# Sparse attention: the product with the sums' reciprocals by ScalarE, a head at a time, in place of VectorE

## The chip, the cores and the metric

One core of a Trainium2 chip runs the whole program. The metric is the device time in microseconds (us) of one execution. Engines: TensorE (PE, its weight loads PEld), VectorE (DVE), ScalarE (ACT), GpSimd (POOL) and SyncE (SP, which only issues DMAs here).

## The reference

The program is a macaron stack: expert layer, sparse attention, expert layer, expert layer, dense attention, expert layer. The change is in the sparse attention. Its core, for 8 batches of 256 tokens, 8 heads of 16 columns:

```python
scores = jnp.einsum('bhqd,bhkd->bhqk', Q, K) * scale
thr = jax.lax.top_k(scores, k)[0][..., k - 1:k]          # k = 25 of 256
masked = jnp.where(scores >= thr, scores, -jnp.inf)
probs = jax.nn.softmax(masked, axis=-1)
attn = jnp.einsum('bhqk,bhkd->bhqd', probs, V)
attn = attn.transpose(0, 2, 1, 3).reshape(B, S, D)
distilled = (attn.reshape(-1, g2) @ Wd.T + bd).reshape(B, S, D)
mixed = gate * distilled + (1.0 - gate) * attn
return mixed @ Wo.T + bo
```

The softmax is not divided before the product with V. V carries a column of ones beside each head's 16, so the product of the unnormalised weights gives a head's 16 sums and, in a 17th column, the sum of its weights. Division by that sum comes last: a reciprocal of 8 columns and a product of 8 x 16 columns by 8 reciprocals. The change is about this product.

## The kernel before, in words

Every engine has its own instruction stream, written out by hand, and waits for others by counting semaphores (dictionary `A` for this attention). An engine takes its stream in order: what waits holds up all behind it.

The attention (`pe_a0`, `act_a0`, `dve_a0`, `pool_a0`) goes in 64 steps `a`: a step is two heads of one half batch (128 queries), four steps make a half batch (`g`), eight a batch `b`. I write r0 to r7 for the steps of a batch (`r = a % 8`). For a step:

- PE computes the scores (`pe_a0_S`, L512), three steps ahead; ACT copies them out of PSUM (`act_a0_c`, L1105).
- DVE searches the 25th largest of each row (`dve_a0_topk`): for each of two heads four MAX8 (L1707) and three MATCH_REPLACE8 (L1709).
- POOL takes the row maximum for the exponential (`pool_a0_negm`, L2082), ACT does the exponential (`act_a0_e`, L1117), POOL the comparison with the threshold and the product (`any_select`, L1732, L1738). In most steps POOL also issues an indirect DMA of the expert layer (L2066 in the first 24 steps; L2051 in 33 to 40, 49 to 56 and from 59).
- PE transposes the weights a step later (L529), ACT copies them (`act_a0_pT`, L1123), PE multiplies them with V two steps later (`pe_a0_PV`, L543) into bank 2 or 3, by the half batch.

The end of a batch is done within the next one. On DVE, `dve_a0_nrm` stands ahead of the search in r1 (first half) and r3 (second half): a reciprocal into the single buffer `rden` (L1716) and the product into `attn` (L1718). On PE, `pe_a0_aT` transposes `attn` in r3 (L555), behind the scores of that step; `pe_a0_ds` in r4 (L560) and `pe_a0_o` in r5 (L566 to L568) give the layer's output. ACT stands between these with `act_a0_aT` (L1127) and `act_a0_mixt` (L1099). DVE adds the output to `x` in r7, ahead of that step's search (`dve_a0_x`, L1723). The next batch's projections run between: q in r2 (L471), k in r3 (L477), V in r4 (L483).

In order, PE's stream in step r3 is: scores of step r6, transposes of `attn`, transposes of step r2's weights, product of step r1, projection k. ACT's is: exponential of r3, copies of the scores of r6, copy of r2's weights, copy of k, copy of the transposed `attn`.

The last batch has its first half's reciprocal and product ahead of the search of step 63, and its second half's behind the last selection.

Of the kernel before, what the change touches and what calls it, by code (L numbers as in the profile page):

```python
# [6 lines left out]
P = 128  # L7
# [4 lines left out]
ACT = mybir.ActivationFunctionType  # L12

B, S, D = 8, 256, 128
# [9 lines left out]
H0, DH0 = 8, 16  # L24
# [35 lines left out]
def build(nc, packed, packed_b, x_in, out):  # L60
    ctx = ExitStack()
    with ctx:
        def sb(name, cols, dt=F32, rows=P):
            return ctx.enter_context(nc.sbuf_tensor(name, [rows, cols], dt))

        def sem(name):
            return ctx.enter_context(nc.semaphore(name))

        def sems(stage, names):
            return {n: sem(f"{stage}_{n}") for n in names.split()}  # L70

        def after(e, s, n):

            if n > 0:
                e.wait_ge(s, n)


        bank = [ctx.enter_context(nc.psum_tensor(f"bank{i}", [P, CN], F32)) for i in range(8)]
# [5 lines left out]
        def cst(name, a=0, b=None, rows=slice(0, P)):  # L84
# [17 lines left out]

        W = {"m0": dict(w1=0, w2=512, b2=768, b1=896, all=900), "m1": dict(w1=0, w2=256, b2=512, b1=640, all=642)}
        tab = {k: nc.dram_tensor(f"tab_{k}", (E * P, W[k]["all"]), F32).ap() for k in W}
        b2d = nc.dram_tensor("b2d", (E, D), F32).ap()

        xsc = nc.dram_tensor("xsc", (AREAS * BS, D), F32).ap()
        ys = nc.dram_tensor("ys", (NBLK * BS, D), F32).ap()
        ws = [sb(f"ws{n}", W["m0"]["all"]) for n in range(SLOTS)]
        xb = [sb(f"xb{n}", BS) for n in range(XSLOTS)]  # L110
# [63 lines left out]
        rden = sb("rden", H0)  # L174
        attn, aT, mixt = (s2b[:, n * S:n * S + S] for n in (0, 1, 3))
# [5 lines left out]
        s_b2d = sem("s_b2d")  # L181
        s_tab = {k: sem("s_tab_" + k) for k in W}
        s_mhalf, s_set, s_setup, s_late_done = (sem(n) for n in ("s_mhalf", "s_set", "s_setup", "s_late_done"))
# [18 lines left out]
        A = sems("a0", "stats mv veps rstd nmr xn T xT q qe k ke V Ve th gp gate S c tk negm e mask p PT pT PV den nrm "  # L202
                       "aT aTe ds wo1 mixt o x")
# [159 lines left out]
        def pe_dense_second(e, u, x_):  # L363
            n, w = u.x0 + x_, W[u.k]["w2"]
            e.wait_ge(F["hb"], u.j0 + 2 * x_ + 2)
            after(e, F["x"], n - 1)
            if x_ < 2:

                after(e, M["ye"], NBLK * u.i)
            for t in range(CT):  # L370
                for a in range(2):
                    i = e.matmul(bank[2 + x_ % 2][:, t * P:t * P + P],  # L372
                                 hbD[:, (2 * x_ + a) % 4 * CN + t * P:(2 * x_ + a) % 4 * CN + t * P + P],
                                 ws[(u.w0 + x_) % SLOTS][:, w + a * D:w + a * D + D], start=a == 0, stop=a == 1)
            i.then_inc(F["y"], 1)
# [30 lines left out]
        def pe_block_second(e, g, n):  # L406
            b = g.first + n
            w = W[g.k]["w2"]
            e.wait_ge(M["hb"], b + 1)
# [85 lines left out]
        def scores(a):  # L495

            return a + min(a, LEAD)
# [49 lines left out]
        def ebank(b):  # L547

            return bank[0 if b == B - 1 else 1]
# [495 lines left out]
        def act_a0_xT(e, b):  # L1045
            e.wait_ge(A["T"], b + 1)
            e.activation(axT[:, :], bank[0][:, 0:S], ACT.Copy, accum_out=xsum[:, :]).then_inc(A["xT"], 1)

        def act_a0_qe(e, b):
            e.wait_ge(A["q"], b + 1)  # L1050
            for n in range(2):
                i = e.activation(qT[b % 2][:, n * S:n * S + S], bank[0][:, n * S:n * S + S], ACT.Identity, bias=cst("a0_bq", n, n + 1))
            i.then_inc(A["qe"], 1)

        def act_a0_ke(e, b):
            e.wait_ge(A["k"], b + 1)
            for n in range(2):
                i = e.activation(kT[b % 2][:, n * S:n * S + S], bank[0][:, n * S:n * S + S], ACT.Identity, bias=cst("a0_bk", n, n + 1))
            i.then_inc(A["ke"], 1)

        def act_a0_xn(e, b):
            e.wait_ge(A["nmr"], 2 * b + 2)
            after(e, A["T"], b)
            for t in range(2):
                i = e.activation(xn[:, t * P:t * P + P], x[:, b * S + t * P:b * S + t * P + P], ACT.Identity,
                                 bias=rstd[:, 2 + t:3 + t], scale=rstd[:, t:t + 1])
            i.then_inc(A["xn"], 1)

        def act_a0_th(e, b):
            e.wait_ge(A["V"], b + 1)  # L1070
            e.activation(gsm[:, 0:1], bank[0][0:64, S:S + 1], ACT.Tanh, bias=bgh[:, 0:1], scale=0.5 / S).then_inc(A["th"], 1)
# [9 lines left out]
        def act_a0_gate(e, b):  # L1081
            e.wait_ge(A["gp"], b + 1)
            g = gate[b % 2]
            e.activation(g[:, 0:1], bank[0][:, 0:1], ACT.Identity, bias=cst("a0_bgp"))
            e.activation(g[:, 1:2], bank[0][:, 0:1], ACT.Identity, bias=gateb[:, 0:1], scale=-1.0)
            e.activation(g[:, 2:3], bank[0][:, 0:1], ACT.Identity, bias=gateb[:, 1:2], scale=cst("a0_bd")).then_inc(A["gate"], 1)
# [14 lines left out]
        def act_a0_c(e, a):  # L1101
            e.wait_ge(A["S"], scores(a) + 1)
            after(e, A["p"], a - 3)
            for j in range(2):
                i = e.activation(sS[:, (a % 4 * 2 + j) * S:(a % 4 * 2 + j + 1) * S], bank[4 + j][:, 0:S], ACT.Copy)  # L1105
            i.then_inc(A["c"], 1)
# [5 lines left out]
        def act_a0_e(e, a):  # L1112
            e.wait_ge(A["negm"], a + 1)
            after(e, A["p"], a - 1)
            for n in range(2):
                q, s = (a % 2 * 2 + n) * S, a % 4 * 2 * S + n * S
                i = e.activation(eS[:, q:q + S], sS[:, s:s + S], ACT.Exp, bias=negm[:, a % 2 * 2 + n:a % 2 * 2 + n + 1], scale=DH0 ** -0.5)  # L1117
            i.then_inc(A["e"], 1)

        def act_a0_pT(e, a):  # L1120
            e.wait_ge(A["PT"], a + 1)
            after(e, A["PV"], a - 1)
            e.activation(pT[:, a % 2 * 2 * S:(a % 2 + 1) * 2 * S], bank[6 + a % 2][:, :], ACT.Copy).then_inc(A["pT"], 1)  # L1123

        def act_a0_aT(e, b):
            e.wait_ge(A["aT"], b + 1)
            e.activation(aT[:, :], ebank(b)[:, 0:S], ACT.Identity, bias=gateb[:, 2:3]).then_inc(A["aTe"], 1)  # L1127
# [21 lines left out]
        def act_a0(e):  # L1149
            for a in range(8 * B):  # L1150
                b, r = a // 8, a % 8
                act_a0_e(e, a)
                if LEAD <= a + 3 < 8 * B:
                    act_a0_c(e, a + 3)
                if a >= 1:
                    act_a0_pT(e, a - 1)
                if b + 1 < B:
                    if r == 0:
                        act_a0_xn(e, b + 1)
                    elif r == 1:  # L1160
                        act_a0_xT(e, b + 1)
                    elif r == 2:
                        act_a0_qe(e, b + 1)
                    elif r == 3:
                        act_a0_ke(e, b + 1)
                    elif r == 4:
                        act_a0_th(e, b + 1)
                    elif r == 5:
                        act_a0_Ve(e, b + 1)
                    elif r == 7:  # L1170
                        act_a0_gate(e, b + 1)
                if r == 7:
                    act_a0_wo1(e, b)
                if b > 0 and r == 3:
                    act_a0_aT(e, b - 1)
                elif b > 0 and r == 4:
                    act_a0_mixt(e, b - 1)
                if a in NORM_A0:
                    act_xn(e, S1.parts[NORM_A0[a]])
                elif a in T_A0:  # L1180
                    act_xnT(e, S1.parts[T_A0[a]])
                elif a in TOP_A0:
                    act_th(e, S1.parts[TOP_A0[a]])
            act_a0_pT(e, 8 * B - 1)
# [524 lines left out]
                    e.match_replace(wk[:, n * S:n * S + S], m8s[:, m:m + 8], s, -3.0e38).then_inc(A["tk"], 1)  # L1709

        def dve_a0_nrm(e, b, g):
            W = DH0 + 1
            o = bank[2 + g][:, 0:H0 * W].rearrange("p (h d) -> p h d", h=H0)
            e.wait_ge(A["PV"], b * 8 + (g + 1) * 4)
            after(e, A["aT"], b)
            e.reciprocal(rden[:, :], o[:, :, DH0]).then_inc(A["den"], 1)  # L1716
            e.wait_ge(A["den"], 2 * b + g + 1)
            e.tensor_tensor(attn[:, g * P:g * P + P].rearrange("p (h d) -> p h d", h=H0), o[:, :, 0:DH0],  # L1718
                            rden[:, :].unsqueeze(2).to_broadcast([P, H0, DH0]), ALU.mult).then_inc(A["nrm"], 1)
# [678 lines left out]
```

## Time and profile before

| | us |
|---|---|
| three runs | 1114.26, 1118.98, 1119.06 |
| median | 1118.98 |
| the profiled execution | 1111.8 |
| its span | 1110.0 |
| DVE busy of the span | 789.5 (71%) |
| PE busy | 951.4 (86%) |
| ACT busy | 571.4 (51%) |
| POOL busy | 459.8 (41%) |

All times of rows are microseconds from the start of the span of the profiled execution, unless marked ns. An engine's instructions overlap a little: the next one starts before the one ahead has ended, so a chain's length is read from start to start. The sparse attention lies at about 190 to 525 us.

### The profile page before, as it was taken

What the parts mean: (1) busy time and instruction counts of PE and PEld (TensorE: products, weight loads), DVE (VectorE), ACT (ScalarE), POOL (GpSimd) and SP (SyncE); (2) the same over time, 40 slices, a digit from 0 to 9 for tenths busy, and PEclk for the clock granted to TensorE, in tenths of its full rate; (3) what the DMA queues carried; (4) which work ended last, traced back from release to release, by engine and by line L of the source; (5) the groups of instructions that cost most, each with busy time, mean ns of one, the idle gap of its engine ahead of it and who ended that gap; (6) DMA issues with size and microseconds to landing.
All of it is one profiled execution on the core that took longest, in us unless ns stands there. A gap on an engine that the chain in (4) does not pass through costs nothing.

```text
span 1110.0 us, 18262 instructions
## 1 busy us (share of the span) xinstructions
PE 951.4 (86%) x5092; PEld 723.8 (65%) x5092; DVE 789.5 (71%) x3096; ACT 571.4 (51%) x1309; POOL 459.8 (41%) x538
## 2 busy tenths in 40 slices
PE   5869979779798898875999785999899999997994
PEld 3538867567576776755995574885566666666963
DVE  5545687999999999995555853346688786864333
ACT  4326655445454544533763451677666766752631
POOL 2530028888757857845004435002522041032034
PEclk9979985555555555555999997999999999998998
DMA  9845613000150000012774313651100000005852
GB/s 306 290 143 148 207 40 134 11 12 15 29 75 8 13 1 6 13 57 91 209 214 139 86 32 94 179 160 34 32 9 1 1 20 2 1 20 151 245 160 61
DMA packets 63444, 95.66 MB, mean 86 GB/s; under 512 B 12128, under 2 KB 41968, under 8 KB 63216
## 3 DMA queue, kind: packets, MB, share of 16 engines
q1 hardware_dynamic: 46256, 71.94, 22.2%
q0 software_dynamic: 6144, 12.60, 3.8%
q10 hardware_dynamic: 10944, 9.97, 2.7%
q8 instruction: 42, 0.69, 0.3%
q14 instruction: 58, 0.48, 0.1%
HBM read 69.94 MB, written 30.83 MB: 91 GB/s over the span
## 4 chain that ended last, share of the span: by engine, by line
PE 43%; POOL 10%; issue 7%; ACT 4%; DVE 4%; another core or an unknown queue 3%; DMA 1%; POOLq 0%; ACTq 0%; SPq 0%; DVEq 0%
PE bank L764 9%; PE bank L403 6%; PE bank L748 5%; PE bank L416 4%; POOL vb L1732 4%; PE bank L360 3%; POOL hb L1738 3%; PE bank L738 3%; PE bank L372 2%; PE bank L732 2%; POOL yg L2066 2%; PE bank L543 1%; PE bank L391 1%; POOL xsc L2051 1%
## 5 line engine op out<-in xcount | busy, mean ns | idle before, releaser
L2066 POOL DMA_INDIRECT yg<-ys,posg x96 | 96.0, 1000 | 144.8 <-DMA ys<-ysb 55.5
L1707 DVE MAX8 vb<-sg 128x8 f32<-128x256 f32 x384 | 146.3, 431 | 0.0
L1732 POOL TENSOR_SCALAR vb<-sS,vb 128x256 f32<-128x256 f32 x126 | 115.2, 925 | 65.0 <-DVE vb L1707 61.6
L2051 POOL DMA_INDIRECT xsc<-xnS,posu x96 | 96.2, 1002 | 63.8 <-DVE posu L1481 35.9
L1117 ACT ACTIVATE hb<-sS,negm 128x256 f32<-128x256 f32 x128 | 58.0, 501 | 120.3 <-POOL negm L2082 119.9
L403 PE MATMUL bank<-xbT,ws 128*128 128x256 f32 x456 | 114.5, 388 | 0.0
L360 PE MATMUL bank<-xnT,ws 128*128 128x512 f32 x192 | 99.2, 646 | 13.6 <-issue 8.7
L543 PEld LDWEIGHTS bank<-kn,qn 128*128 128x128 f32 x512 | 107.0, 308 | 0.0
L1709 DVE MATCH_REPLACE8 sg<-vb,sg 128x256 f32<-128x256 f32 x256 | 104.9, 426 | 0.0
L543 PE MATMUL bank<-kn,qn 128*128 128x17 f32 x512 | 101.4, 338 | 0.0
L372 PEld LDWEIGHTS bank<-ws,hb 128*128 128x128 f32 x512 | 67.2, 206 | 49.7 <-issue 38.1
L372 PE MATMUL bank<-ws,hb 128*128 128x128 f32 x512 | 69.9, 291 | 32.5 <-issue 16.0
L529 PE MATMUL bank<-pk,hb 128*128 128x128 f32 x256 | 66.7, 413 | 35.3 <-POOL hb L1738 33.9
L403 PEld LDWEIGHTS bank<-xbT,ws 128*128 128x128 f32 x456 | 82.7, 195 | 9.3 <-issue 0.7
L529 PEld LDWEIGHTS bank<-pk,hb 128*128 128x128 f32 x256 | 47.5, 215 | 58.2 <-POOL hb L1738 48.6
L416 PEld LDWEIGHTS bank<-ws,hbM 128*128 128x128 f32 x608 | 79.3, 192 | 6.3 <-issue 1.7
L512 PE MATMUL bank<-zacc,exb 16*128 16x256 f32 x240 | 68.9, 669 | 15.9 <-ACT sS L1105 13.4
L1738 POOL TENSOR_TENSOR hb<-vb,hb 128x512 f32<-128x512 f32 x63 | 79.8, 1267 | 5.2
L1839 DVE SCALAR_TENSOR_TENSOR zacc<-bank,rden,zacc 128x128 f32<-128x128 f32 x256 | 78.0, 347 | 5.1
L416 PE MATMUL bank<-ws,hbM 128*128 128x128 f32 x608 | 79.7, 275 | 0.8 <-DVE ysb L1581 0.8
L764 PEld LDWEIGHTS bank<-VO,sS 128*128 128x128 f32 x512 | 63.1, 198 | 24.2 <-issue 15.1
L764 PEld LDWEIGHTS bank<-VO,hb 128*128 128x128 f32 x512 | 60.3, 191 | 24.5 <-issue 16.0
(226 smaller groups left out, 1913.3 us busy)
## 6 DMA issues: line engine op xcount, KB each, us to landing
ws<-tab_m SPq DMA_DIRECT2D x46, 450.0 KB, 3.7
ws<-tab_m SPq DMA_DIRECT2D x54, 321.0 KB, 3.4
xb<-xsc SPq DMA_DIRECT2D x76, 128.0 KB, 2.7
ys<-ysb ACTq DMA_DIRECT2D x76, 128.0 KB, 3.4
xsc<-qn SPq DMA_DIRECT2D x3, 2048.0 KB, 10.7
pk<-packed SPq DMA_DIRECT2D x1, 3209.0 KB, 10.4
tab_m<-packed SPq DMA_DIRECT2D x5, 512.0 KB
ws<-packed SPq DMA_DIRECT2D x8, 256.0 KB, 4.6
```

Of the source, the lines that this page charges most:

```text
L360: i = e.matmul(u.hid(j, s)[:, :], w[:, f:f + P], xnT[:, chunk(u.c)], start=True, stop=True)
L372: i = e.matmul(bank[2 + x_ % 2][:, t * P:t * P + P], hbD[:, (2 * x_ + a) % 4 * CN + t * P:(2 * x_ + a) % 4 * CN + t * P + P], ws[(u.w0 + x ...
L403: i = e.matmul(g.hid(b, s, a), w[:, f:f + P], xbT[b % 2][:, :], start=True, stop=True)
L416: i = e.matmul(bank[2 + b % 2][:, t * P:t * P + P], hbM[:, half(b)][:, a * BS + t * P:a * BS + t * P + P], ws[(g.w0 + n) % SLOTS][:, w + a ...
L529: i = e.transpose(bank[6 + a % 2][:, n * P:n * P + P], pS[:, q:q + P], cst("ident"))
L543: i = e.matmul(bank[2 + g][:, h * W:h * W + W], pT[:, q:q + P], V0[p][:, (t * H0 + h) * W:(t * H0 + h + 1) * W], start=t == 0, stop=t == 1)
L764: i = e.matmul(bank[n % 2][:, j * W1:j * W1 + W1], AT[g % 2][:, a:a + P], VO[:, (2 * h + t) * W1:(2 * h + t + 1) * W1], start=t == 0, stop ...
L1707: e.max(m8s[:, m:m + 8], s).then_inc(A["tk"], 1)
L1732: i = e.tensor_scalar(msk[:, n * S:n * S + S], sS[:, s:s + S], m[:, n, TOPK - 1:TOPK], None, ALU.is_ge)
L1738: e.tensor_tensor(pS[:, q], msk[:, :], eS[:, q], ALU.mult).then_inc(A["p"], 1)
L2051: e.indirect_dma_start(xsc[:, :], at(posu[g.p], t, k), xnS[:, g.tile(t)], None).then_inc(s_sc, 16)
L2066: e.indirect_dma_start(yg[:, y:y + D], None, ys[:, :], at(posg[g.p], t, k)).then_inc(s_g[t % GY], 16)
```

## The change

Of the 16 half batches, 15 have their product done by ACT, in eight instructions of 128x16 (a head each), with the head's reciprocal as the per-partition scale. DVE keeps all 16 reciprocals and the product of the last half batch. On ACT the eight stand behind the exponential and the score copies of r1 (first half) and r3 (second half) of the next batch, and behind the exponential of step 63 for the last batch's first half. The reciprocal, which waited for the transposes of the batch before (`aT`), now waits until the product ahead of it has read `rden` (`nrm`).

```diff
+        def act_a0_nrm(e, b, g):
+            W = DH0 + 1
+            e.wait_ge(A["den"], 2 * b + g + 1)
+            after(e, A["aT"], b)
+            for h in range(H0):
+                i = e.activation(attn[:, g * P + h * DH0:g * P + (h + 1) * DH0], bank[2 + g][:, h * W:h * W + DH0], ACT.Copy,
+                                 scale=rden[:, h:h + 1])
+            i.then_inc(A["nrm"], 1)
...
                 act_a0_e(e, a)
                 if LEAD <= a + 3 < 8 * B:
                     act_a0_c(e, a + 3)
+                if b > 0 and r == 1:
+                    act_a0_nrm(e, b - 1, 0)
+                elif b > 0 and r == 3:
+                    act_a0_nrm(e, b - 1, 1)
+                elif a == 8 * B - 1:
+                    act_a0_nrm(e, b, 0)
                 if a >= 1:
                     act_a0_pT(e, a - 1)
...
             e.wait_ge(A["PV"], b * 8 + (g + 1) * 4)
-            after(e, A["aT"], b)
+            after(e, A["nrm"], 2 * b + g)
             e.reciprocal(rden[:, :], o[:, :, DH0]).then_inc(A["den"], 1)
+            if 2 * b + g + 1 < 2 * B:
+                return
+            e.wait_ge(A["aT"], b)
             e.wait_ge(A["den"], 2 * b + g + 1)
             e.tensor_tensor(attn[:, g * P:g * P + P].rearrange("p (h d) -> p h d", h=H0), o[:, :, 0:DH0],
                             rden[:, :].unsqueeze(2).to_broadcast([P, H0, DH0]), ALU.mult).then_inc(A["nrm"], 1)
```

DVE's stream around r3 of the fifth batch (step 35), before; L1716 and L1718 are the reciprocal and the product of the batch before, the rest is search:

```order
L1707 MAX vb<-sg 128x8 x2
L1716 RECIPROCAL rden<-bank 128x8
L1718 TENSOR_TENSOR s2b<-bank,rden 128x128
L1707 MAX vb<-sS 128x8 x2
L1709 MATCH_REPLACE sg<-vb,sS 128x256 x2
```

The same place in the changed kernel, whose lines have other numbers (L1733 the reciprocal, L1723 and L1725 the search):

```order
L1723 MAX vb<-sg 128x8 x2
L1733 RECIPROCAL rden<-bank 128x8
L1723 MAX vb<-sS 128x8 x2
L1725 MATCH_REPLACE sg<-vb,sS 128x256 x2
L1723 MAX vb<-sg 128x8 x2
```

The product is gone between the reciprocal and the search's first MAX.

ACT's stream in r3, as a piece of the difference; L1131 is the new product, L1117 the exponential, L1105 the score copies, L1123 the copy of the weights, L1058 that of k, L1127 (now L1137) that of the transposed `attn`:

```order
 L1117 ACTIVATE hb<-sS,negm 128x256 x2
 L1105 ACTIVATE sS<-bank 128x256 x2
+L1131 ACTIVATE s2b<-bank,rden 128x16 x8
 L1123 ACTIVATE qn<-bank 128x512
 L1058 ACTIVATE zacc<-bank,pk 128x256 x2
-L1127 ACTIVATE s2b<-bank,gateb 128x256
+L1137 ACTIVATE s2b<-bank,gateb 128x256
```

The eight instructions stand behind two exponentials and two copies, and ahead of the copies that PE's later products need. PE's and POOL's streams are as they were.

## Rows read from the trace of the kernel before

**Rows 1.** Windows: stretch, its length, busy time (count) of each engine, granted clock, DMA.

```profile
190.00:525.00 335.00, 275.62 (x1210) 220.79 (x1211) 323.47 (x1349) 152.12 (x417) 244.78 (x299) 0.54 0.11 27
351.56:366.75 15.19, 15.05 (x61) 12.32 (x60) 15.19 (x64) 7.22 (x19) 13.07 (x16) 0.50 0.04 13
```

**Rows 2.** Timeline, DVE, from r3 of the fifth batch: start, length, instruction, count.

```profile
347.49 0.22 DVE L1716 RECIPROCAL rden<-bank 128x8 f32<-128x8 f32 x1
347.74 0.29 DVE L1718 TENSOR_TENSOR s2b<-bank,rden 128x128 f32<-128x128 f32 x1
347.95 0.74 DVE L1707 MAX8 vb<-sS 128x8 f32<-128x256 f32 x2
...
367.80 0.47 DVE L1723 TENSOR_TENSOR x<-bank,x 128x256 f32<-128x256 f32 x1
```

**Rows 3.** Timeline, ACT, r3 of the fifth batch.

```profile
353.24 0.63 ACT L1105 ACTIVATE sS<-bank 128x256 f32<-128x256 f32 x2
353.77 0.59 ACT L1123 ACTIVATE qn<-bank 128x512 f32<-128x512 f32 x1
```

**Rows 4.** Timeline, PE, the same batch: transposes of attn, last output products.

```profile
351.56 0.69 PE L555 MATMUL bank<-pk,s2b 128*128 128x128 f32 x2
...
366.12 0.63 PE L568 MATMUL bank<-pk 128*128 128x128 f32 x2
```

**Rows 5.** Timeline, ACT, small instructions and their successors, 368 and 376 us.

```profile
368.04 0.44 ACT L1076 ACTIVATE kn<-bank 128x128 f32<-128x128 f32 x2
368.35 0.29 ACT L1079 ACTIVATE gsm<-gsm,bgh 64x1 f32<-64x1 f32 x1
...
376.01 0.28 ACT L1085 ACTIVATE gate<-bank,gateb 128x1 f32<-128x1 f32 x1
376.15 0.38 ACT L1086 ACTIVATE gate<-bank,gateb,pk 128x1 f32<-128x1 f32 x1
376.39 0.43 ACT L1092 ACTIVATE vb<-pk,gate 128x128 f32<-128x128 f32 x1
376.68 0.52 ACT L939 ACTIVATE xnS<-x,rstdM 128x128 f32<-128x128 f32 x1
```

**Rows 6.** Timeline, second batch: PE's last output products, DVE's addition.

```profile
229.10 0.63 PE L568 MATMUL bank<-pk 128*128 128x128 f32 x2
233.06 0.41 DVE L1723 TENSOR_TENSOR x<-bank,x 128x256 f32<-128x256 f32 x1
```

**Rows 7.** Timeline, fourth batch, the same two.

```profile
321.22 0.63 PE L568 MATMUL bank<-pk 128*128 128x128 f32 x2
325.34 0.45 DVE L1723 TENSOR_TENSOR x<-bank,x 128x256 f32<-128x256 f32 x1
```

**Rows 8.** Timeline, sixth batch: score copies, transposes, last output products, addition.

```profile
396.66 0.65 ACT L1105 ACTIVATE sS<-bank 128x256 f32<-128x256 f32 x2
396.08 0.69 PE L555 MATMUL bank<-pk,s2b 128*128 128x128 f32 x2
410.64 0.63 PE L568 MATMUL bank<-pk 128*128 128x128 f32 x2
413.41 0.45 DVE L1723 TENSOR_TENSOR x<-bank,x 128x256 f32<-128x256 f32 x1
```

**Rows 9.** Timeline, eighth batch: last output products, addition.

```profile
499.19 0.63 PE L568 MATMUL bank<-pk 128*128 128x128 f32 x2
508.24 0.46 DVE L1723 TENSOR_TENSOR x<-bank,x 128x256 f32<-128x256 f32 x1
```

**Rows 10.** Timeline, POOL, fifth batch: step r4's product of mask and exponentials.

```profile
360.00 1.27 POOL L1738 TENSOR_TENSOR hb<-vb,hb 128x512 f32<-128x512 f32 x1
```

**Rows 11.** Timeline, the attention's end: POOL and ACT.

```profile
508.46 1.82 POOL L1732 TENSOR_SCALAR vb<-sS,vb 128x256 f32<-128x256 f32 x2 [0.29 <-DVE vb L1707]
517.17 0.96 POOL L2051 DMA_INDIRECT xsc<-xnS,posu  x1 [0.30 <-issue]
516.70 0.60 ACT L1123 ACTIVATE qn<-bank 128x512 f32<-128x512 f32 x1 [1.84 <-PE bank L529]
```

## The prediction

> **What bounds the kernel now.** I read the windows first: between 190 and 525 us, where the sparse attention lies, DVE is busy for 323.5 of 335.0 us, PE for 275.6, POOL for 244.8, ACT for 152.1 [rows 1]. DVE has work without a gap up to the end of its last search; so an instruction taken from it is worth its whole pitch, and a wait put on it costs its whole length. Then I read one batch on each engine by its timeline, from r3 to r7: what DVE and PE hand each other there is the second thing that bounds. The reader is to see in [rows 2 to 4] a chain that runs beside DVE: the transposes of `attn` on PE start at 351.56 (L555), the last output product starts at 366.12 and ends at 366.75 (L568), and DVE's addition of that output starts at 367.80 (L1723). DVE comes 1.05 us after its data there. PE is busy for 15.05 of the 15.19 us between [rows 1]: the way from the transposes to the output is PE's own queue, with no idle time that could take up a delay.
>
> **What goes from DVE.** Between the reciprocal's start and the next search there are 347.95 - 347.49 = 0.46 us for reciprocal and product [rows 2]. The product waits for the reciprocal's result (0.25 us from start to start); without it the next search starts at the reciprocal's own pitch, its length less the overlap. The product shows that overlap: it lasts 0.29 and its successor starts 0.21 after it, 0.08 less; I take 0.22 - 0.11 = 0.11 us, an estimate with the larger overlap that I see between searches. So 0.35 us go each time (at least 0.21, the product's pitch alone). 14 of the 15 products that go stand ahead of the last selection on POOL; the 15th stands ahead of search 63, at the very end, where DVE later waits anyway and where I count nothing. 14 x 0.35 = 4.9 us (2.9 at the least).
>
> **What ACT gets.** Eight instructions of 16 columns with one pointer operand (the scale), out of PSUM. The trace has none like it. Pitches nearby, from start to start [rows 5]: one column with one pointer 0.14 (L1085), one column with two pointers 0.24 (L1086), 128 columns with a scale pointer 0.29 (L1092), 128 columns without a pointer 0.155 (L1076, two in 0.31). Copies of 256 columns without a pointer have 0.265 (two in 0.53, [rows 3]), so 128 columns more cost 0.11. That brings L1092 down to 0.20 for 16 columns and L1085 up to 0.155. I take 0.18, between the two: the last ends about 0.11 later than its pitch, so a group takes 8 x 0.18 + 0.11 = 1.55 us, and 0.05 more until PE starts. The ends are 8 x 0.14 + 0.11 = 1.2 and 8 x 0.29 + 0.13 = 2.45.
>
> The Trainium skill (ScalarE: Activation LUTs, What ACT_TABLE_LOAD costs) gives 186 ns plus 0.833 ns a column, 93 ns for each pointer and 93 ns of overlap; by it the group would be 8 x 0.199 + 0.09 = 1.7 us and the sum below 0.7 us more. L1076's two in 0.44 us are less than the 0.49 that this gives for them, so the trace has a bit less. The same page's rules for kernel authors say to multiply on VectorE and not on ScalarE; the rows side with that as far as work goes (0.46 us with the reciprocal on DVE against some 1.5 on ACT), and it would matter only where ACT is waited for, as below.
>
> ACT has the time: 15 groups are 23 us on an engine that idles for 183 us of this stretch [rows 1]. What matters is who waits behind a group.
>
> **In r1** nobody does. The first half's product may come late up to r2's product on PE (which refills the bank) and r3's reciprocal on DVE, and the fifth batch's timeline has both of them well behind the place where the group would end. Cost: nothing.
>
> **In r3** PE's transposes of `attn` need the second half's product. Before, DVE had it done at 348.0 and PE came to it at 351.56, when its own queue let it [rows 2, 4]. Now it comes behind ACT's exponential and score copies of r3, which have to wait for that step's maximum: the copies start at 353.24, the next instruction at 353.77 [rows 3]. The group runs from 353.77 to 355.32, PE starts at 355.37: 3.81 us later than before. Behind the waiting transposes on PE are all its further work: transposes of r2's weights, product, projection k, scores of r7, and so on up to the output. The order holds all of it by 3.81 us, and PE has nothing to shorten it with. The output ends at 366.75 + 3.81 = 370.56; DVE would be at its addition at 367.80 - 0.35 = 367.45. DVE waits for 3.1 us, where it never waited.
>
> Batch by batch, delay of PE less slack at the addition, plus what DVE comes earlier:
> - second and third batch: the same delay of 3.81 (pattern of the fifth); the output ended at 229.73 and DVE came at 233.06, slack 3.33 [rows 6], the third the same within 0.01: 3.81 - 3.33 + 0.35 = 0.83 us each.
> - fifth: 3.1, as above. Seventh: the same within 0.02.
> - sixth: PE is late there too; the score copies are only 0.58 behind PE's transposes, where they were 1.68 behind in the fifth. The group starts at 396.66 + 0.53 = 397.19, PE at 398.79 instead of 396.08, delay 2.7; slack 413.41 - 411.27 = 2.14 [rows 8]. ACT's place is set there by PE and not by DVE's last search, so both of DVE's savings (r1 and r3) go off the slack: 2.7 - 2.14 + 0.7 = 1.3.
> - fourth: the pattern and the delay of the sixth, 2.7; slack 325.34 - 321.85 = 3.49 [rows 7]; 2.7 - 3.49 + 0.7 = -0.1: none.
> - eighth: slack 508.24 - 499.82 = 8.4 [rows 9], no delay gets through.
>
> Sum of waits: 2 x 0.83 + 3.1 + 3.1 + 1.3 = 9.1 us. The scores for the searches run three steps ahead (some 15 us), so a delay of 3.81 us does not reach DVE by them.
>
> POOL is held too: the exponential of r4 stands behind ACT's copies of k and of the transposed `attn`, which come later by PE's delay, so it would end at about 362.4 by my estimate, where POOL's product started at 360.00 [rows 10]. That is 2.4 us. In the fifth and seventh batch DVE's own wait of 3.1 covers it; in the second and third POOL has to win it back up to the next r3, from small gaps. I count nothing, and 1 us at most.
>
> **At the end** POOL's selection of step 62 and its last scatter (508.46, 517.17) follow DVE, and with them the blocks of the next layer. ACT's group behind the exponential of step 63 delays the copy of step 62's weights, but step 63's copy waits for PE until 516.70 in any case [rows 11], after the group is over. Nothing there.
>
> **Sum:** -4.9 + 9.1 = +4.2 us. The profiled execution took 1111.8 (span 1110.0), so the like of it takes 1116.0. The median of the three runs is 7.2 us above the profiled execution, for no reason that the rows show; from it I get 1118.98 + 4.2 = 1123.2 us.
>
> **Rivals.**
> 1. *Cheap waits, the saving stays.* PE would catch up between transposes and output, or DVE would reach the addition later than I say, and the 3.81 us vanish. Then -4.9 us: 1114.1. For it: DVE's stretch is full and ACT is idle half of the time. Against it: [rows 1], 15.05 of 15.19 us busy, and the slack of 1.05 us in two batches. Half of the waits missing gives -0.3, no difference.
> 2. *The group is long*, slower beyond doubt. Its place is ACT's r3, its price the instruction: with 0.24 us a head (two pointers' pitch) the group is 2.05 us, half a us more in five batches and 0.4 in the fourth, total +7.1; at 0.29 it is 2.45 and 0.9 us more in five, 0.8 in the fourth: +9.5, 1128.5. It becomes slower by over 0.5% (5.6 us) from 0.21 us a head on. For it: the nearest row with this very operand (scale pointer) is the 0.29. Against: it has 128 columns.
> 3. *POOL's delay is carried along.* In the steps with an indirect DMA POOL is nearly full (0.29 us of idle time ahead of a selection, [rows 11]). If the 2.4 us of the fourth step are not recovered, the next r3 starts later and its wait grows: 1 to 3 us more over all batches, +5 to +7.
>
> **How the numbers follow.** Forecast (+3 to +5.6) 0.50; rival 1 or a part of it (-4.9 to +3) 0.20; rival 2 0.20; rival 3 0.10. What a measurement of this kernel can tell from no change is about 0.5%, 5.6 us: the forecast is within it. Slower by more: rival 2 nearly whole and half of rival 3, and some scatter of the forecast, since two of the shown runs differ by 4.8 us: 0.35. Faster by more needs the whole of rival 1 and luck: 0.04. No change: 0.61. The range reaches from rival 1 to rival 2: 1113 to 1128, with a us below for the scatter; the forecast's own is 1122 to 1125.
>
> **What would show it.** In the changed profile: DVE busy about 4.5 us less; new instructions L1131 x120 with 0.18 us from start to start and some 0.29 us long; idle time of PE ahead of L555 by ACT, about 3.8 us in four batches and 2.7 in two; idle time of DVE ahead of its addition by PE, 9 us in five batches, 3 us each in the fifth and seventh; the attention's end 4 us later, and all after it unchanged in length. Wrong if DVE never waits ahead of the addition (rival 1), if L1131 is above 0.21 us a head (rival 2), or if the exponential of r3 comes later after the end of DVE's search of r2 than now (rival 3).

## The result: 0.5% slower

| | before | changed |
|---|---|---|
| median of 20 runs each | 1118.95 us | 1123.93 us |
| lowest, highest | 1113.72, 1121.06 | 1118.68, 1128.76 |
| profiled execution's span | 1110.0 | 1116.6 |

The ratio is 1.0051, with a 95% interval of 1.0035 to 1.0067: slower by some 5 us (4.2 were forecast).

In the attention's stretch the engines' busy times, to be laid beside [rows 1] (columns as there):

```profile
190.00:525.00 335.00, 277.01 (x1198) 224.48 (x1197) 316.63 (x1327) 171.57 (x535) 243.66 (x296) 0.52 0.12 26
```

In these 335 us DVE has 6.8 us less of busy time and ACT 19.5 us more. Over the whole span DVE has 5.1 us less (784.4 against 789.5); the rest of the 6.8 is work that now lies outside these 335 us. Who waits for whom on DVE in the stretch (columns: engine, line, what it waited for, us in total, times, longest):

```profile
DVE x L1743 <- PE bank L568: 8.1, 5, 2.9
DVE rden L1733 <- PE bank L543: 4.4, 1, 4.4
DVE lg L1421 <- PE bank L317: 0.8, 1, 0.8
```

The second row was there before, at the stage's end. The first is new: the addition of the output (L1723 before, L1743 now) waits in five batches. And on PE:

```profile
PE bank L555 <- ACT s2b L1131: 14.3, 3, 7.1
PE bank L555 <- issue: 13.2, 5, 3.7
```

L555 are the transposes of `attn`. The first row is the second, third and eighth batch (the 7.1 is the eighth). Of the five with "issue", for which the profile names no releaser, one (0.7 us) belongs to the last batch, whose second product DVE still does. The other four are the fourth to seventh batch, where PE's stream has a wait for the expert layer just ahead of the one for the group. That these four wait for the group too is shown by the experiments below: they shrink with the group's length and are gone when it comes early.

The fifth batch, on ACT, PE and DVE, to be laid beside [rows 2 to 4] (timeline: start, length, instruction, count, idle time before it):

```profile
349.73 0.64 ACT L1105 ACTIVATE sS<-bank 128x256 f32<-128x256 f32 x2
350.25 1.43 ACT L1131 ACTIVATE s2b<-bank,rden 128x16 f32<-128x16 f32 x8
353.33 0.60 ACT L1123 ACTIVATE qn<-bank 128x512 f32<-128x512 f32 x1 [1.65 <-PE bank L529]
```

```profile
351.78 0.66 PE L555 MATMUL bank<-pk,s2b 128*128 128x128 f32 x2 [3.66 <-issue]
352.24 1.06 PE L529 MATMUL bank<-pk,hb 128*128 128x128 f32 x4
...
366.31 0.61 PE L568 MATMUL bank<-pk 128*128 128x128 f32 x2
```

```profile
344.00 0.19 DVE L1733 RECIPROCAL rden<-bank 128x8 f32<-128x8 f32 x1
344.10 0.70 DVE L1723 MAX8 vb<-sS 128x8 f32<-128x256 f32 x2
...
366.96 0.42 DVE L1743 TENSOR_TENSOR x<-bank,x 128x256 f32<-128x256 f32 x1 [2.92 <-PE bank L568]
```

The group ends at 351.68, PE starts its transposes 0.10 us later after 3.66 us of idle time, from there to the output's end it takes 15.1 us as before, and DVE, which was at its addition 2.92 us earlier, waits. From DVE's reciprocal to its addition it is 22.96 us, where it was 20.31.

To compare kernels without what varies outside the stretch I use two marks on DVE: the first reciprocal (step r1 of the second batch) and the one ahead of search 63. Between them lie all effects but the fifteenth product's. Before: 200.10 to 508.56, 308.46 us; changed: 198.25 to 510.53, 312.28 us, so 3.8 us more.

### The profile page after: what moved, and what is told of

Read it like the earlier page. It is cut to its first block, busy times and chain, and to the rows that moved or that the text cites. A ratio compares the mean times of both kernels' runs of the same rounds, so it can differ in the third digit from the quotient of the medians.

```text
span 1116.6 us, 18382 instructions
## 1 busy us (share of the span) xinstructions
PE 959.9 (86%) x5092; PEld 733.1 (66%) x5092; DVE 784.4 (70%) x3081; ACT 592.3 (53%) x1429; POOL 460.3 (41%) x538
## 4 chain that ended last, share of the span: by engine, by line
PE 54%; DVE 15%; issue 8%; POOL 8%; another core or an unknown queue 6%; ACT 6%; DMA 2%; SPq 0%; POOLq 0%; ACTq 0%; DVEq 0%
PE bank L403 9%; PE bank L764 9%; PE bank L416 6%; PE bank L360 5%; PE bank L748 4%; DVE vb L1723 4%; DVE sg L1725 4%; PE bank L372 3%; POOL vb L1752 3%; POOL hb L1758 3%; PE bank L738 2%; PE bank L543 2%; PE bank L732 2%; PE bank L391 2%
## 5 line engine op out<-in xcount | busy, mean ns | idle before, releaser
L1723 DVE MAX8 vb<-sg 128x8 f32<-128x256 f32 x384 | 142.9, 413 | 0.0
L543 PEld LDWEIGHTS bank<-kn,qn 128*128 128x128 f32 x512 | 110.9, 318 | 0.0
L543 PE MATMUL bank<-kn,qn 128*128 128x17 f32 x512 | 105.1, 346 | 0.0
L1117 ACT ACTIVATE hb<-sS,negm 128x256 f32<-128x256 f32 x128 | 57.9, 501 | 88.9 <-POOL negm L2102 88.9
L1725 DVE MATCH_REPLACE8 sg<-vb,sg 128x256 f32<-128x256 f32 x256 | 102.7, 408 | 0.0
L764 PEld LDWEIGHTS bank<-VO,hb 128*128 128x128 f32 x512 | 61.7, 195 | 25.8 <-issue 17.1
L764 PEld LDWEIGHTS bank<-VO,sS 128*128 128x128 f32 x512 | 63.3, 198 | 23.0 <-issue 12.4
```

The source lines that it names most:

```text
L543: i = e.matmul(bank[2 + g][:, h * W:h * W + W], pT[:, q:q + P], V0[p][:, (t * H0 + h) * W:(t * H0 + h + 1) * W], start=t == 0, stop=t == 1)
L764: i = e.matmul(bank[n % 2][:, j * W1:j * W1 + W1], AT[g % 2][:, a:a + P], VO[:, (2 * h + t) * W1:(2 * h + t + 1) * W1], start=t == 0, stop ...
L1723: e.max(m8s[:, m:m + 8], s).then_inc(A["tk"], 1)
```

## The experiments

All edits are shown against the changed kernel. The marks and the waits are read from one profile each; the ratio compares whole runs with runs of the kernel before on the same chip. "Second halves only" has 6 runs, "group twice" only 4.

| kernel | marks, us | waits ahead of the additions, us (times) | ratio to before (95%) |
|---|---|---|---|
| before | 308.46 | 0 | |
| changed | 312.28 | 8.1 (5) | 1.0051 (1.0035 to 1.0067) |
| first halves only | 306.52 | 0 | 0.9986 (0.9962 to 1.0010) |
| second halves only | 315.44 | 7.7 (5) | 1.0094 (1.0061 to 1.0127) |
| group in r2 | 304.04 | 0 | 0.9963 (0.9939 to 0.9987) |
| one copy for eight | 308.14 | 3.6 (2) | 1.0017 (0.9996 to 1.0038) |
| PE's order | 303.47 | 0 | 0.9943 (0.9919 to 0.9968) |
| group twice | 320.80 | 16.2 (6) | 1.0116 (1.0074 to 1.0158) |
| both cures | 303.44 | 0 | 0.9982 (0.9962 to 1.0001) |
| changed again | 313.84 | 8.1 (5) | 1.0067 (1.0043 to 1.0092) |

**Which half costs.** First the first halves alone:

```diff
-            if 2 * b + g + 1 < 2 * B:
+            if g == 0:
                 return
...
-                elif b > 0 and r == 3:
-                    act_a0_nrm(e, b - 1, 1)
```

> Only the first halves' products (r1) go to ACT; the second halves' stay on DVE in r3. Between DVE's reciprocal in r1 of the second batch and its reciprocal ahead of search 63 it was 308.5 us before and 312.3 in the changed kernel. My theory (PE waits for ACT's group in r3, its queue carries that to the output, DVE waits for it in r7): no wait ahead of DVE's additions, seven products saved at 0.35 us, 306.0 us between the marks, time 2.5 us below before. Rival, that ACT's extra work itself slows the stretch wherever it stands: about half of the loss stays, some 310 us, time 2 us above before.

306.52 us between the marks, 1.9 less than before, and no wait ahead of an addition. The 0.5 us above my 306.0 is in the seven products that stay: they start 0.28 to 0.31 us after their reciprocal, where it was 0.22 to 0.25. The time is within 0.5% of before, with an interval of -0.4% to +0.1%. The rival, ACT's extra work wherever it stands, is out: seven groups in r1 put no wait on DVE.

Then the second halves alone:

```diff
-            if 2 * b + g + 1 < 2 * B:
+            if g == 1 and b < B - 1:
                 return
...
-                if b > 0 and r == 1:
-                    act_a0_nrm(e, b - 1, 0)
-                elif b > 0 and r == 3:
+                if b > 0 and r == 3:
                     act_a0_nrm(e, b - 1, 1)
-                elif a == 8 * B - 1:
-                    act_a0_nrm(e, b, 0)
```

> Only the second halves' products (r3) go to ACT; the first halves' stay on DVE. My theory: all of the waits ahead of DVE's additions stay, some 7.5 to 8 us (8.1 in the changed kernel, less a little because DVE comes 0.35 us later to two of them), seven products saved; 313.7 us between the marks, time 5.4 us above before, worse than the full change. Rival, that the loss goes with the amount of ACT's work: half of it, 310 us, 2 us above before.

The waits in its profile:

```profile
DVE x L1739 <- PE bank L568: 7.7, 5, 2.9
DVE x L1611 <- DMA yg<-ys,posg: 2.9, 1, 2.9
DVE pos L1482 <- PE bank L329: 0.8, 1, 0.8
```

7.7 us as expected, and worse than the full change, between the marks by 3.2 us. It is 1.7 us more than I expected there; 1.0 of it are small waits of the expert layer's routing (the third row, and 0.2 at another line), and some 0.5 the later start of the products that stay, as above. The wait for the gather (second row) lies ahead of the first mark and belongs to this one profile. The ratio, 1.0094, is above the 1.0048 that I expected, and its interval (from 1.0061) leaves that out; of this excess I have no explanation but the variation outside the marks (below), and six runs.

**Where the group stands.** On ACT, the second half's group moves from r3, behind the exponential and the score copies, to r2:

```diff
-                elif b > 0 and r == 3:
-                    act_a0_nrm(e, b - 1, 1)
...
                 if a >= 1:
                     act_a0_pT(e, a - 1)
+                if b > 0 and r == 2:
+                    act_a0_nrm(e, b - 1, 1)
```

> All products as in the change, but the second half's group stands on ACT in r2, behind the copy of the weights and ahead of q's copy, instead of behind r3's exponential and score copies. My theory: the group is over before PE comes to the transposes of attn (within 0.5 us), no waits ahead of the additions, the whole saving of 14 x 0.35 us stays: 303.6 us between the marks, time 4.9 us below before. Rival, amount of ACT's work: as the changed kernel, 312 us, 5 us above before. Rival, POOL's delay by the late exponential is what costs: here the exponentials of r4 are on time as well, so it expects the same as my theory.

304.04 us, 4.4 less than before, no wait ahead of an addition, ratio 0.9963. The same work on ACT is now a gain. (Of the 5.0 us that the products are worth, 0.6 goes into a wait of DVE for the routing's logits.) In the fifth batch (ACT, then PE):

```profile
345.80 1.43 ACT L1131 ACTIVATE s2b<-bank,rden 128x16 f32<-128x16 f32 x8
347.05 0.91 ACT L1052 ACTIVATE exb<-bank,pk 128x256 f32<-128x256 f32 x2
348.90 0.91 ACT L1117 ACTIVATE hb<-sS,negm 128x256 f32<-128x256 f32 x2 [0.94 <-POOL negm L2102]
```

```profile
348.04 0.69 PE L555 MATMUL bank<-pk,s2b 128*128 128x128 f32 x2
```

The group ends at 347.23, and PE comes to its transposes at 348.04 without a wait. What held the group in r3 was mostly not its own length: the exponential of r3 starts at 348.90, after PE wants the result.

**How much is the group's own length.** One copy stands for the eight, at the same places; the products with the reciprocals are left out for 15 of the 16 halves.

```diff
-            for h in range(H0):
-                i = e.activation(attn[:, g * P + h * DH0:g * P + (h + 1) * DH0], bank[2 + g][:, h * W:h * W + DH0], ACT.Copy,
-                                 scale=rden[:, h:h + 1])
+            i = e.activation(attn[:, g * P:g * P + P].rearrange("p (h d) -> p h d", h=H0),
+                             bank[2 + g][:, 0:H0 * W].rearrange("p (h d) -> p h d", h=H0)[:, :, 0:DH0], ACT.Copy)
```

> At the places of the change ACT does one copy of 128x128 without a scale in place of the eight instructions: the products with the reciprocals are left out for 15 of 16 halves. It takes about 0.28 us instead of 1.43. My theory: PE's delay in r3 falls from 3.66 to about 2.5 us (the exponential and the score copies ahead of the group are the larger part), waits of 1.8 us in the fifth and seventh batch and none in the second, third and sixth, 307.8 us between the marks, time 0.6 us below before. Rival, that the eight instructions' length is the whole loss: no waits, 303.6 us, 4.9 us below before.

```profile
DVE x L1742 <- PE bank L568: 3.6, 2, 1.8
DVE lg L1420 <- PE bank L317: 1.3, 1, 1.3
DVE pos L1485 <- PE bank L329: 0.8, 1, 0.8
```

PE's wait ahead of the transposes in the fifth batch is 2.52 us instead of 3.66 (in the fourth and sixth 1.42 instead of 2.57), the copy lasts 0.27 us, and two waits of 1.8 us are left, as worked out; 308.14 us against 307.8 expected. (The second and third row are small waits for the routing that I had not counted; against them stands an instruction of 128x4 in the third batch, `rstdM`, that lasts 0.20 us where it was 0.89 before.) The rival, that the eight instructions' length is the whole loss, is out: it had no waits. The ratio, 1.0017, cannot be told from 1 (0.6 us below before was expected).

The other way, the group of r3 is doubled, the first eight writing into an unused place:

```diff
+            if g == 1:
+                for h in range(H0):
+                    e.activation(s2b[:, 2 * S + h * DH0:2 * S + (h + 1) * DH0], bank[2 + g][:, h * W:h * W + DH0], ACT.Copy,
+                                 scale=rden[:, h:h + 1])
             for h in range(H0):
```

> The change with the second half's group of eight preceded by eight of the same into an unused place, so the group of r3 takes 1.26 us more. By the measured 0.157 us from start to start: PE's delay 4.9 us in five batches, waits of 1.26 us more in each of the second, third, fifth, sixth and seventh batch and about 1.1 in the fourth: 15.5 us ahead of the additions, 319.7 us between the marks, time 7.4 us above the changed kernel (12.5 above before). A rival that has slack left in r3 expects less than half of that.

```profile
DVE x L1747 <- PE bank L568: 16.2, 6, 4.2
DVE lg L1425 <- PE bank L317: 0.8, 1, 0.8
DVE pos L1490 <- PE bank L329: 0.8, 1, 0.8
```

16.2 us of waits (15.5 expected), now in the fourth batch as well (1.09 us), 320.8 us between the marks (319.7 expected). PE waits 4.9 us ahead of the transposes in four batches (not five, as I wrote) and 3.9 in the fourth and sixth. The group is longer by some 1.3 us, and each of the six waits grows by 1.1 to 1.6: past the slack, a longer group costs about its length. The median is 13.7 us above before (12.5 expected).

**Who carries the delay.** ACT is left as in the change; PE's transposes of `attn` move to the end of its stream in r3, behind projection k.

```diff
-                if b > 0 and r == 3:
...
-                    pe_a0_aT(e, b - 1)
-                elif b > 0 and r == 4:
+                if b > 0 and r == 4:
...
                     elif r == 6:
                         pe_a0_gp(e, b + 1)
+                if b > 0 and r == 3:
...
+                    pe_a0_aT(e, b - 1)
```

> ACT exactly as in the change; on PE the transposes of attn move from ahead of step r2's weights to the end of r3's stream, behind projection k. If the loss is what stands behind the waiting transposes on PE: PE waits for the group in none of the seven batches but the eighth (which has no projections), no waits ahead of DVE's additions, 304.0 us between the marks as with the group in r2 (304.0 measured), time 4.5 us below before. If the loss is ACT's place or work itself, it stays at 312 us and 5 us above before.

```profile
351.56 1.43 ACT L1131 ACTIVATE s2b<-bank,rden 128x16 f32<-128x16 f32 x8
```

```profile
349.34 1.12 PE L529 MATMUL bank<-pk,hb 128*128 128x128 f32 x4
350.25 1.73 PE L543 MATMUL bank<-kn,qn 128*128 128x17 f32 x8
351.82 2.05 PE L477 MATMUL bank<-axT,pk 128*128 128x256 f32 x4
353.67 0.64 PE L555 MATMUL bank<-pk,s2b 128*128 128x128 f32 x2
```

```profile
DVE rden L1733 <- PE bank L543: 4.4, 1, 4.4
```

ACT's group is as late as in the change (it ends at 352.99), but PE has its other work of r3 ahead of it and comes to the transposes at 353.67, without a wait. DVE's only wait of the stretch is the one at its end, which was there before. 303.47 us, 5.0 less than before, ratio 0.9943, the lowest of all. So it is not ACT's lateness by itself that costs, but what stands behind the waiting transposes on PE.

**Both cures together**, the group in r2 and PE's order:

> Group in r2 on ACT and PE's transposes of attn at the end of r3. Each cure alone should already take away all the waits, so both together expect no more: 304.0 us between the marks, 4.5 us below before. If the time outside the marks (which differed by up to 9 us between single profiles) hangs on something of this order, it would show here as a difference from the kernel with the group in r2 alone.

303.44 us between the marks, as with PE's order alone. The ratio was 0.9982, though (some 2 us below before, where 4.5 were expected), against 0.9943 and 0.9963 with one cure. The stretch is the same within 0.6 us, so these three tell how far the comparison of whole runs is to be trusted: about 0.2% either way.

**The change once more, unaltered:**

> The changed kernel once more, unaltered, on this chip with the others: 312.3 us between the marks within 0.5 us, 8.1 us of waits ahead of the additions, and time 4 to 6 us above before. It tells how far the stretch outside the marks varies from profile to profile.

8.1 us of waits once more; 313.84 us, 1.6 more than the first profile, which misses my bound of 0.5. 1.4 of it are two waits for the routing's rank products that the first profile lacked:

```profile
DVE pos L1486 <- PE bank L329: 1.4, 2, 0.8
```

They lie in the fourth and the sixth batch, and there PE's granted clock differs between the two profiles: for 3 us behind the output it was 1.00 and 0.81 in the first and 0.50 in both in the second. The fourth batch, first and second profile (columns: stretch, length, PE busy, granted clock, DMA):

```profile
322.40:325.40 3.00, 3.00 (x27) 1.00 0.00 0
325.66:328.66 3.00, 3.00 (x15) 0.50 0.00 0
```

Eight of the 17-column products (L543) take 0.96 us there in the first and 1.73 in the second; the difference, 0.8, is about the length of such a wait (0.63 and 0.76). That the clock makes the waits is not shown by a run of its own.

The ratio, 1.0067, agrees with the first, 1.0051.

**What varies outside the marks.** In the dense attention, from the start of the first 512-column projection (L732) to the start of the last L764 that reads `hb`, the ten profiles take 260.4 to 268.6 us: 260.4 before, 263.0 changed, 263.9 changed again, 268.2 with PE's order. The instructions there are the same in all. Of the 6.6 us between the spans of before and changed, 3.8 lie between the marks, 2.6 in the dense attention, 2.1 behind it, and -1.9 ahead of the first mark.

The length goes with PE's granted clock. The same 30 us (50 to 80 us behind that first projection) before, changed, and with PE's order:

```profile
793.60:823.60 30.00, 26.65 (x156) 1.00 0.09 23
795.50:825.50 30.00, 26.92 (x153) 0.94 0.09 23
792.90:822.90 30.00, 25.40 (x137) 0.89 0.09 23
```

Before, the clock is at its upper level all the way between 50 and 190 us. Four profiles (changed, changed again, second halves, both cures) have it at the lower level once, for some 3.5 us, and take 263.0 to 264.0. The five others have it there for some 7 us and once more for 3.5, and take 266.6 to 268.6. What makes it fall in one execution and not in another these runs do not show; changed and changed again, the one kernel that was profiled twice, have the same fall. The profile of before is the one with no fall, and it is 7 us faster than that kernel's median, so the 2.6 us cannot be put down to the change.

## Why the prediction was right

- **DVE's saving.** 0.35 us a product, 4.9 in all. With PE's order the stretch falls into 14 intervals from reciprocal to reciprocal, each 0.30 to 0.40 us shorter than before, 5.0 in all. The next search starts 0.10 after the reciprocal (0.11 taken).
- **The group's length.** 0.18 a head was taken between 0.155 and 0.20; it is 0.157 (in the second batch the first starts at 214.55 and the eighth at 215.65). 1.43 us instead of 1.55. Of the two rows that I stood between, the one with one column was right, although its pointer was a bias and this one is a scale. That was the term mis-sized, by 0.12 us a group.
- **PE's delay.** 3.81 and 2.7 forecast, 3.62 to 3.66 (four batches) and 2.57 (two) measured, shorter mostly by the group's error. My list of what the profile would show left out the eighth batch, where PE waits 7.07 us; that it costs nothing was right: DVE's addition had no wait there.
- **DVE's waits.** Forecast 0.83, 0.83, 0, 3.1, 1.3, 3.1, 0, in sum 9.1; measured 0.55, 0.55, 0, 2.92, 1.17, 2.94, 0, in sum 8.1. The slack of each batch, read from two rows, told the five batches that wait from the two that do not.
- **POOL.** Its product of step r4 came late as forecast: in the fifth batch 14.88 us after DVE's reciprocal of r3, where it was 12.51 [rows 2, 10], 2.4 us later. DVE's own wait of 2.92 us is longer than that:

```profile
354.19 1.83 POOL L1752 TENSOR_SCALAR vb<-sS,vb 128x256 f32<-128x256 f32 x2 [0.27 <-DVE vb L1723]
358.88 1.28 POOL L1758 TENSOR_TENSOR hb<-vb,hb 128x512 f32<-128x512 f32 x1 [2.86 <-issue]
```

  Rival 3 is out. Its sign was to be a later start of r3's exponential and copies after the end of r2's search: the score copies of the fifth batch start 5.73 us after the reciprocal (5.75 before, [rows 2, 3]), and the wait did not grow from the second batch to the third (0.55 both) nor from the fifth to the seventh (2.92, 2.94). In the second batch POOL's product of r4 is 1.6 us later after the reciprocal and that of r7 0.5.
- **Sum.** +4.2 forecast. Between the marks -5.0 + 8.1 + 0.8 = +3.9, measured +3.8. The 0.8 is a wait of DVE for the routing's logits (L1421), which I had not seen coming; 0.6 of it stays with the group in r2, and it is gone with PE's order. Why is not shown. The `rstdM` instruction of the third batch, 0.17 us against 0.89 before, goes the other way. So the sum closes to some tenths of a us, and leaves no more than that for POOL. That the forecast is as near as 0.4 us is in part luck: 1.0 us too much in the waits, and this 0.8 left out.
- **The whole time.** 1123.93 against 1123.2 forecast is nearer than the method can promise. The prediction had all behind the attention unchanged in length; in the two profiles it is 4.7 us longer, by what varies outside the marks, and the profiled execution took 1118.77 where I had 1116.0.
- **Rival 1** (the saving stays) is what the kernel does once either cure is in. **Rival 2** needed 0.21 us a head; the instruction has 0.157.

## What to carry to other kernels

Work taken from the busiest engine is only as good as the place it gets on the other: the idle engine was idle because its stream waits for others, and what is put behind such a wait comes when the wait ends. Ask what the consumer's queue holds behind it, and read, batch by batch, the slack between the consumer's last output and the one who needs it; here two rows a batch gave the waits within 1 us (9.1 against 8.1). Either cure kept the saving here: put the work ahead of the wait in its own stream, or the consumer's dependent step behind its independent ones.

## What I had not expected of the hardware

Eight small ACT instructions in a row overlap by half: each lasts 0.304 us (median of 120) and the next starts 0.157 after it. The Trainium skill (ScalarE: Activation LUTs, What ACT_TABLE_LOAD costs) gives 93 ns of overlap; an estimate from its figures is a length of 186 + 13 + 93 = 292 ns and 199 from start to start. The length agrees within 4%, the overlap does not: 147 ns were measured.

PE's granted clock rises behind the output in some batches and not in others, and the idle time ahead of the transposes does not tell which. In the fifth batch of the changed kernel it rose in spite of 3.66 us of idle time in r3 (columns as above):

```profile
352.00:366.00 14.00, 13.86 (x55) 0.50 0.03 10
367.20:370.20 3.00, 3.00 (x27) 1.00 0.06 22
```

It is at the lower level (1.2 GHz) up to the output and at the upper (2.4 GHz) behind it, and eight L543 take 0.96 us from 367.20 on. Before, without the idle time, they took 0.96 from 367.34 on. But over the seven batches, in the 3 us behind each output, the clock was raised in all seven before (0.87 to 1.00), in the fourth to seventh in the changed kernel, in the second, third, fifth and seventh in its second profile, and in the second, sixth and seventh with PE's order, where PE has no idle time ahead of the transposes in any batch but the eighth. What decides it is open.
